# A chunked gated delta rule with FFN on one core: inverse and scaled keys brought back from DRAM together, and a new order of the engines' work

## What is computed

```python
# attention part
lam = sigmoid(lam_logit); beta = eta * (1.0 - lam) / d          # d = 16
x_act = tanh(x)
static_out = einsum('bld,ed->ble', x_act, W)
q = k = to_heads(x_act); v = to_heads(static_out)
# per (batch, head), a scan over the 2048 positions:
#   S = lam * S;  u = beta * (v_t - S^T k_t);  S += k_t u^T;  o_t = S^T q_t
y = static_out + o
attn = layernorm(y) * ln_gamma + ln_beta
x = layernorm(x + attn)
# ffn part, weights are integers times 1/127
h = silu(x @ wg.T) * (x @ wu.T)
x = layernorm(x + h @ wd.T)
```

## Time and profile before

| | |
|---|---|
| median of 3 executions | 1783.09 us |
| the profiled execution, its own time | 1788.68 us |
| its span, first to last instruction | 1786.9 us |
| mean granted clock of TensorE | 0.845 of full speed |
| TensorE busy | 1389.4 us, 78% |
| VectorE busy | 1401.8 us, 78% |
| ScalarE busy | 1104.0 us, 62% |
| GpSimd busy | 793.8 us, 44% |
| DMA queue of SP | 700816 packets, 187.56 MB, 49.9% of 16 engines |

### The profile page before, as it was taken

The page is one execution under the profiler, slowest core; times in us unless marked ns, Lnnn a source line. Parts: engine busy times, 40 slices in busy tenths (PEclk is TensorE's granted clock), DMA queues, the critical chain, the costliest instruction groups (busy, mean ns, idle before and its releaser), DMA issues.

```text
span 1786.9 us, 53677 instructions
## 1 busy us (share of the span) xinstructions
PE 1389.4 (78%) x21032; PEld 1077.5 (60%) x21032; DVE 1401.8 (78%) x3461; ACT 1104.0 (62%) x2357; POOL 793.8 (44%) x1106
## 2 busy tenths in 40 slices
PE   4357878888878888888888888788888887788764
PEld 3245666666666666666666666666666666666542
DVE  5478878878878888888878888888888887888741
ACT  3236667666667666666666666667666666666544
POOL 6023454444444454444444444444453444445442
PEclk9657888878888898888888988889888888989877
DMA  5555545545555555555445556654555554455200
GB/s 122 104 107 112 110 114 118 109 99 114 121 105 116 112 112 110 115 125 125 102 115 115 108 103 121 121 108 114 114 106 107 122 121 105 113 117 106 58 24 24
DMA packets 701069, 190.98 MB, mean 107 GB/s; under 512 B 620688, under 2 KB 688272, under 8 KB 700816
## 3 DMA queue, kind: packets, MB, share of 16 engines
q1 hardware_dynamic: 700816, 187.56, 49.9%
HBM read 103.55 MB, written 67.11 MB: 96 GB/s over the span
## 4 chain that ended last, share of the span: by engine, by line
PE 31%; SPq 20%; DMA 16%; DVE 15%; ACT 9%; issue 6%; POOL 1%; ACTq 0%; POOLq 0%; DVEq 0%
PE pc L181 10%; PE pd L278 5%; SPq L948 5%; SPq L957 4%; SPq L991 4%; DMA scr_t<-t 4%; PE pu L252 4%; PE pf L215 4%; PE pg L252 3%; SPq L1004 3%; DMA scr_x<-xt 3%; ACT v L684 3%; PE pf L226 2%; DMA y_out<-v 2%; DMA scr_g<-gs 2%
## 5 line engine op out<-in xcount | busy, mean ns | idle before, releaser
L885 POOL TENSOR_TENSOR hlo<-gate,hhi 128x512 f16<-128x512 f32 x192 | 228.6, 1193 | 326.8 <-ACT hhi L716 326.4
L181 PE MATMUL pc<-R,tb 128*128 128x32 f16 x4096 | 158.1, 189 | 153.8 <-DVE R L368 135.0
L181 PEld LDWEIGHTS pc<-R,tb 128*128 128x128 f16 x4096 | 147.5, 118 | 172.1 <-DVE R L368 149.6
L181 PE MATMUL pc<-S,e 128*128 128x32 f16 x4096 | 157.3, 187 | 66.4 <-DVE S L389 66.2
L181 PEld LDWEIGHTS pc<-S,e 128*128 128x128 f16 x4096 | 151.9, 118 | 83.2 <-DVE S L389 75.4
L278 PE MATMUL pd<-wd_t,hhi 128*128 128x256 f16 x768 | 176.9, 277 | 13.6 <-DVE xr L487 8.1
L181 PEld LDWEIGHTS pc<-U,kb 128*128 128x128 f16 x4096 | 154.1, 118 | 51.5 <-DVE U L376 49.1
L215 PEld LDWEIGHTS pf<-xb,e 128*128 128x128 f16 x4096 | 152.3, 117 | 46.8 <-DMA e<-scr_x 28.7
L181 PE MATMUL pc<-U,kb 128*128 128x32 f16 x4096 | 159.6, 190 | 25.5 <-DVE U L376 25.5
L278 PE MATMUL pd<-wd_t,hlo 128*128 128x256 f16 x768 | 176.7, 276 | 0.0
L215 PE MATMUL pf<-xb,e 128*128 128x32 f16 x4096 | 156.3, 192 | 23.3 <-DMA e<-scr_x 21.6
(11 more groups left out here) (124 smaller groups left out, 3281.9 us busy)
## 6 DMA issues: line engine op xcount, KB each, us to landing
xa<-L_attn_x SPq DMA_DIRECT2D x128, 128.0 KB
scr_x<-xt SPq DMA_DIRECT2D x64, 256.0 KB, 2.1
xb<-scr_x SPq DMA_DIRECT2D x256, 64.0 KB, 2.9
e<-scr_x SPq DMA_DIRECT2D x256, 64.0 KB, 3.6
scr_g<-gs SPq DMA_DIRECT2D x32, 512.0 KB
gh<-scr_g SPq DMA_DIRECT2D x32, 512.0 KB, 3.9
kb<-k SPq DMA_DIRECT2D x512, 32.0 KB, 2.2
scr_t<-t SPq DMA_DIRECT2D x64, 256.0 KB, 4.4
```

Source lines behind the costliest of these rows:

```text
L181: last = pe.matmul(pc2[:, :, cols], stationary(h, a), moving[:, :, cols], start=a == 0, stop=a == 1)
L885: pool.tensor_tensor(hlo[:, t, :], gate[:, t % 2, :], hhi[:, t, :], ALU.subtract).then_inc(SEM["hl"], 1)
```

## The change

1. tb and kb become two halves of one tensor tk, and scr_t becomes scr_tk with a part for the inverse and a part for the scaled keys. The scaled keys are stored to DRAM (`sp_store_scaled`), and one transfer of 64 KB per batch and half brings inverse and scaled keys back together (`sp_load_blocks`). TensorE waits for the one semaphore ahead of the inverse product.
2. The solver's partitions hold (head, batch) instead of (batch, head). With that the gram's store has pieces of 256 bytes over 128 partitions and its load contiguous rows of 4096 bytes; before it was the other way.
3. The order of all five engines is written anew. The first four gate tiles and the first two up tiles of the FFN run one step earlier, within windows 2 and 3; the inversion, scaled keys and the stores of the inverse are moved within the step or into the step before; SP's list is rearranged.

The diff, cut to its core, with a line or two of each order:

```diff
-        tb = sb("tb", [P, 2, H, B, C, 2, 2], F16)
-        kb = sb("kb", [P, 2, H, B, DH, 2, 2], F16)
+        tk = sb("tk", [P, 2, 2, H, B, C, 2, 2], F16)
+        tb, kb = tk[:, :, 0], tk[:, :, 1]
...
-        scr_g = nc.dram_tensor("scr_g", [C, B + 1, H, T], F32).ap()[:, 0:B]
-        scr_t = nc.dram_tensor("scr_t", [2, B, H, C, T], F16).ap()
+        scr_g = nc.dram_tensor("scr_g", [H, B, C, T], F32).ap()
+        scr_tk = nc.dram_tensor("scr_tk", [2, 2, H, B, C, T], F16).ap()
...
         def pe_inverse_by_rest(pe, q, p, w):
             pe.wait_ge(SEM["r"], n_of("r", q, w + 1))
             if w % 2 == 0:
-                pe.wait_ge(SEM[f"tb{w // 2}"], n_of(f"tb{w // 2}", q))
+                pe.wait_ge(SEM[f"tk{w // 2}"], n_of(f"tk{w // 2}", q))
...
         def pe_keys_by_update(pe, q, p, w):
-            if w % 2 == 0:
-                pe.wait_ge(SEM[f"kb{w // 2}"], n_of(f"kb{w // 2}", q))
...
         def pe_step(pe, s, p):
             if live(s - 2):
-                pe_up(pe, s - 2, p, 0)
-                pe_gate(pe, s - 2, p, 0)
...
+                pe_gate(pe, s - 2, p, 4)
                 pe_up(pe, s - 2, p, 2)
...
         def act_scale_keys(act, q, p, g):
-            act.wait_ge(SEM[f"kb{g}"], n_of(f"kb{g}", q - 1))
+            act.wait_ge(SEM[f"kd{g}"], n_of(f"kd{g}", q - 1))
...
         def sp_store_gram(sp, q, p):
-            sp.dma_start(scr_g.rearrange("i b h t -> b i (h t)"),
-                         gs[:, :, :, :].rearrange("p h j n -> p (h j n)")).then_inc(SEM["gd"], 16)
+            sp.dma_start(scr_g.rearrange("h b i t -> (b i) h t"),
+                         gs[:, :, :, :].rearrange("p h j n -> p h (j n)")).then_inc(SEM["gd"], 16)
         def sp_load_gram(sp, q, p):
-            sp.dma_start(gh[:, :, :, :].rearrange("p i j n -> p i (j n)"),
-                         scr_g.rearrange("i b h t -> (b h) i t")).then_inc(SEM["gh"], 16)
+            sp.dma_start(gh[:, :, :, :].rearrange("p i j n -> p (i j n)"),
+                         scr_g.rearrange("h b i t -> (h b) (i t)")).then_inc(SEM["gh"], 16)
...
-        def sp_load_inverse(sp, q, p, g):
...
-        def sp_load_kb(sp, q, p, g):
...
+        def sp_store_scaled(sp, q, p, g):
             sp.wait_ge(SEM["k16"], n_of("k16", q, g + 1))
             sp.sem_inc(s_hop, 1)
+            sp.wait_ge(SEM[f"tk{g}"], n_of(f"tk{g}", q - 1))
+            sp.dma_start(scr_tk[g, 1].rearrange("h b i t -> (b i) h t"),
+                         k16[:, g].rearrange("p h k z m -> p h (k z m)")).then_inc(SEM[f"kd{g}"], 16)
+
+        def sp_load_blocks(sp, q, p, g):
+            if q == 0:
+                sp.wait_ge(s_pool0, 15)
+                sp.sem_inc(s_hop, 1)
+            sp.wait_ge(SEM[f"kd{g}"], n_of(f"kd{g}", q))
+            sp.sem_inc(s_hop, 1)
             sp.wait_ge(SEM["sp"], n_of("sp", q - 1, 2 * g + 2))
+            sp.sem_inc(s_hop, 1)
+            sp.wait_ge(SEM[f"td{g}"], n_of(f"td{g}", q))
             for b in range(B):
+                sp.dma_start(tk[C * b:C * (b + 1), g, :, :, b].rearrange("j a h i z m -> j (a h) (i z m)"),
+                             scr_tk[g, :, :, b].rearrange("a h j t -> j (a h) t")).then_inc(SEM[f"tk{g}"], 16)
...
+            act_scale_keys(eng, 0, 0, 0)
+            act_scale_keys(eng, 0, 0, 1)
+            act_square(eng, 0, 0)
             all_steps(eng, act_step)
...
+            dve_scale_keys(eng, 0, 0, 0)
+            dve_scale_keys(eng, 0, 0, 1)
             all_steps(eng, dve_step)
```

322 lines of the change are left out of this document (152 added, 170 removed).

## The result

The changed kernel takes 1831.86 us (median of 4 runs, 1829.91 to 1838.14); the kernel before, in the same rounds on the same chip, 1784.69. The ratio is 1.027, with an interval of 1.0225 to 1.0311: **2.7% slower**. The forecast of 1746 had the sign wrong, and 1832 lies above its range, and above the price of each rival. The profiled execution took 1831.29, its span 1829.5, 42.6 us more than that of before. Of all runs in this document one is left out of the comparisons: one of the four of the kernel called both took 3581.79 us, while the other three lie between 1839.64 and 1847.76.

A forecast was written before the change was run, and what follows sets the result against it. No engine was full; an order bound the kernel, its loop closed by the keys' transfers. Period 51.7 to 50.6 us over 31 periods gives 34, plus 3 at the end: 1783 - 37 = 1746 us, range 1728 to 1766.

The forecast's parts named there:

- The keys' loop: Loop through xt's stores, spread keys, gram and windows back to xt; said to close the old period, forecast at 50.5 us.
- W0: Window from window 3's complete state to window 0's, holding FFN and gram products; forecast 15.95 us, from 20.95.
- W1: Window from window 0's complete state to window 1's; forecast 10.2 us, from 10.5.
- W2: Window from window 1's complete state to window 2's; VectorE becomes the bound, forecast 11.1 us, from 8.4.
- W3: Window from window 2's complete state to window 3's; VectorE bound, forecast 13.1 us, from 11.3.
- The sum of VectorE's loop: The four windows' forecasts added, 15.95 + 10.2 + 11.1 + 13.15 = 50.4 us a period.
- What the data in flight adds to the landing: Residual loads straight ahead of the stores of xt lengthen their landing by 0 to 1 us, 0.5 taken.
- D: Theory from choosing the runs, not the prediction: GpSimd beside VectorE's store of the inverse; no size given.
- rival 2: Residual's 512 KB in flight holds the stores of xt by over 1 us; period 51.7, about 1780 us; chance 0.17.
- It costs nothing at either bound: Gram's store and load, 7.8 to 10.7 us, 9 taken, with x loads between them in an existing wait, delay nothing.
- rival 3: Scaled keys' stores in 128-byte pieces hold the queue if each takes over 4.4 us; about 1817 us; chance 0.15.
- rival 4: TensorE at half clock in W0 for gate 4 and up 2, adding 1.7 to 2.0 us; 1802 us; chance 0.08.

The follow-up runs named there:

- both: Changed kernel with x loads behind the gram's load and residual loads ahead of the gram's store, bias addition in window 0: 1841.79 us, ratio 1.0311.
- residual_gap: combined with residual loads between the inverse's first-half store and its blocks' load, bias addition behind the rest of window 0: 1739.34 us, ratio 0.9717.
- quarter_residual2: combined with only one of four residual loads in each chunk but the first, computing with stale data: 1730.78 us, ratio 0.9678.
- hole_x_transpose: hole plus x loads behind the gram's load and the first keys transpose behind window 2's inverse product: 1773.65 us, ratio 0.9954.
- hole: Changed kernel with the four residual loads issued behind the two stores of xt instead of ahead of them: 1824.91 us, ratio 1.0254.
- combined: hole_x_transpose with the inverse's second-half store on VectorE ahead of the grams, as in store_moved: 1768.0 us, ratio 0.989.
- store_moved: Changed kernel with VectorE's store of the inverse's second half moved from behind the first two grams to ahead of them: 1826.48 us, ratio 1.0213.
- residual_late: Changed kernel with residual loads moved from ahead of xt's stores to ahead of the gram's store, bias addition to window 0: 1855.51 us, ratio 1.0369.
- path_only: Kernel before with only the new data path and solver layout, all engines in the old instruction order: 1785.8 us, ratio 0.9989.
- x_behind_gram: Changed kernel with the four x loads behind the gram's load instead of ahead of it: 1801.31 us, ratio 1.0077.

## Why the prediction was wrong

**What bounds the kernel before**: right. The keys' loop closed its period, and the room for a new order was there (residual_gap has a period of 50.3).

**The windows' sums**: right where nothing waits for a transfer. W0 summed to 15.95 and measured 15.8 (quarter_residual2), with the inverse product 10.4 behind the state for 10.5; W1 10.2 and 10.2; W2 11.1 and 11.1 (hole_x_transpose); W3 13.1 (its terms give 13.0) and 12.8. The sum of VectorE's loop, 50.4, stands beside 50.0.

**The step that failed first**: "What the data in flight adds to the landing is between 0 and 1; I take 0.5". The stores of xt took 3.6 at the median for 2.1, and 5.0 in the chain for the 2.74 of the earlier trace rows: 1.5 to 2.3 more, outside its bounds. The reason given was that loads are issued more slowly than they drain. It took SP's time for the cost of the transfer; with the same 512 KB behind them instead of ahead (hole), the stores took 2.1. With this, from xt to the gram is 811.09 - 793.55 = 17.5 us, for 16.2 forecast. Moving or thinning this load, with the store of the inverse moved, is worth up to 2.0 us of W0 (17.8 to 15.8), of which D is 0.5 once e is early and the half clock another 0.5. Thinning it to a quarter gave 37 us in the same rounds (combined to quarter_residual2). This was rival 2, with the right mechanism and place, but priced at 1780: it took the period of before as its ceiling, as though the loop could not become longer than the old one.

**The second failed step**: "It costs nothing at either bound" of the gram. Its store landed in 3.3, better than the 3.9 of the lower bound. But the x loads were counted by their 2.6 us of issuing alone, "in a wait that was there". SP may issue them only after the key norms (768.37, while the gram's store came out at 766.71), and then their 512 KB went ahead of the gram's: 7.31 and 7.4 for 3.3. From the gram's store to its landing it took 778.35 - 766.71 = 11.6 us, for 9 taken. The store itself went out 11.1 behind the state for 8.9, so the gram is back 22.7 behind it, where 16.7 to 19.6 was forecast. In the kernel before the gram's load stood ahead of the x loads, which the order of rows showed. No rival had this case; "the mask waiting for gh" stood only in the list of signs. It cost 31 to 34 us, about as much as the residual's place.

**The third, not in the working at all**: the first transpose of keys ahead of the inverse product of W2. The sum of W2 follows VectorE alone and has no term for the transpose, nor for what it waits for. It cost 0.4 us in W2 (11.5 to 11.1), and 11 to 12 us in all.

**The fourth**: VectorE's durations were taken from places where GpSimd was not in the way: the store of the inverse as 0.6, where L444 took 1.67 in W0. It cost nothing clear of noise in the changed kernel (store_moved) and 0.5 us a period once the transfers were mended.

**Two loops that lie together.** The prediction saw the keys' loop at 50.0 to 50.5 and VectorE's at 50.4, and treated delays in the first as covered up to 0.4. In the chain above, the loop of the period runs gram to state 15.5, W1 11.0, state to xt 9.35, xt to gram 17.5: 53.4, for 15.1, 10.2, 9.0 and 16.2 forecast, 50.5. Each delay is in series with the others. With no slack, several small terms held to be "in time" needed a joint bound and not one each.

**The scaled keys' stores** (rival 3): 5.2 us each, above the 4.4 from which it was to decide, and yet no loss: the second is issued 0.5 us behind the first (784.02 and 784.52), and both have landed 6.1 us after the first issue, so they land side by side and not one after the other, and the stores of xt are at 2.1 with them in place (residual_late). The threshold was wrong, and the rival fell (path_only, residual_late). Their bounds of 2.7 to 6.8 held; the value taken, 3.9, was too low. The blocks: 3.0 each and hardly waited for, as said. On the rule that small pieces are slow where DRAM takes part (the Trainium skill, DMA: Bandwidth & Descriptors, Why small descriptors are slow (HBM only)) the runs decide less than it seems. The blocks' loads land as xb does, 3.0 for 2.8, but both are in pieces of 128 bytes. The stores take 5.2, but they go out 0.7 us behind the output's four stores, whose last lands at 786.8; the first of them lands 1.9 us after that and the second 3.3. How much of the 5.2 is the small pieces is not shown.

**A cold TensorE** (rival 4): in part there. Half clock costs up to 0.5 us of W0 in the changed kernel, as shown behind its table of windows, for the 1.7 to 2.0 of the rival. The wait that the rival named, ahead of the last inverse product, did bring half clock (748.82 to 752.23, behind a wait of 2.49 us), but on up 1 and gate 3 in W3, where VectorE binds; gate 4 and up 2 take 0.38 a matmul again. With the same TensorE order and e early, the clock in W0 is full in all 27 middle chunks of quarter_residual2.

**Start and end**: the end gave 1.6 us, within the bounds. The start cost 7.7, for nothing forecast; in x_behind_gram it is 3.9 (118.6 for 114.7), so half of it is the same load of the gram. The rest was not tried.

**The sum.** From the changed kernel to residual_gap the ratio falls from 1.0268 to 0.9717, 98 us: x ahead of the gram 34 us (to 1.0077), the residual ahead of xt 10 (to 1.0022), the transposes 12 (to 0.9954), the store of the inverse 11 (to 0.989; 6 by the medians), and 31 the residual's second move together with the bias's move on VectorE (to 0.9717). Each step is a difference of two ratios with intervals of 5 to 8 us to either side, so the smaller ones are rough. The parts are in this sequence; in another each would weigh otherwise, as the three runs show that mended one alone and gained little or lost (residual_late, hole, store_moved).

## What to carry to other kernels

Before moving a bulk load, write down for each transfer of the loop which bytes stand ahead of it in the queue, and for each instruction of the new order what it waits for itself. The load's issue time was the smaller part of its price here (2.6 us of issuing, 4.1 of landing for the gram). Put bulk loads where nothing behind them is awaited soon, and where several terms are "just in time" in one loop, bound their sum. When a change has a data path and an order, run the path in the old order once: here that one run put the loss on the order.

## What the runs showed of the hardware

- Landing times grow with the data ahead. A load of 512 KB took 3.3 us with nothing issued just ahead of it and 7.4 behind 512 KB of x; with the x loads straight behind it, it still took 3.3 (x_behind_gram). A store of 256 KB took 2.1, and 3.6 behind the residual, up to 5.0 in the chain; the gram's store of 512 KB took 3.3, and 5.8 behind the residual.
- A store of 256 KB into DRAM in pieces of 128 bytes landed in 5.0 to 5.7 us, one of as many bytes in long pieces in 2.1. The first always stood straight behind 512 KB of output, so the pieces are not shown to be the cause. The stores that followed 7 to 8 us later were not slowed by them (2.1, 2.2).
- VectorE's 128x512 instruction with two inputs took 1.67 us for 0.68 when GpSimd's subtraction had begun just before it. Where GpSimd's began only 0.08 us before VectorE's end (744.67, in the kernel before), it took 0.67.
- The granted clock of TensorE was half from 759.06 to 762.47, behind a wait of 1.15 us, and three matmuls of gate and up, which take 0.38 us each at the full clock, took 0.51 to 0.63 there.
